# Feature attention in a fused decoder: the mixing cut into halves that stand between single heads, and the maxima's rows turned two heads earlier

## What is computed

```python
qh = layernorm(x).reshape(B, 8, 8, 256)          # B = 32
kh = vh = ctx.reshape(B, 8, 8, 256)
a  = einsum('bhdq,bhdk->bhqk', qh, kh) * 8 ** -0.5
p  = softmax(a, axis=-1)
y  = einsum('bhqk,bhdk->bhdq', p, vh).reshape(B, 64, 256)
x  = x + selu(einsum('oc,bct->bot', W, y))
```

## Time and profile before

| | us |
|---|---|
| median of 3 runs | 1336.93 |
| lowest, highest | 1335.71, 1339.19 |
| the profiled execution | 1332.79 |
| its span, first to last instruction | 1330.7 |
| mean granted TensorE clock | 0.974 |

### The profile page before, as it was taken

One profiled execution on the slowest core, in us unless ns is written; L12 is line 12 of the kernel. 1 busy time (PEld: TensorE's weight loads), 2 busy tenths in 40 slices (PEclk: granted clock), 3 DMA queues, 4 the chain that ended last, 5 costly groups with the idle time before them and its releaser, 6 DMA issues. The chain is left out here.

```text
span 1330.7 us, 27523 instructions
## 1 busy us (share of the span) xinstructions
PE 1215.3 (91%) x9976; PEld 963.9 (72%) x9976; DVE 958.9 (72%) x1862; ACT 709.2 (53%) x1475; POOL 454.5 (34%) x537
## 2 busy tenths in 40 slices
PE   4999988988888779798899999999997999999998
PEld 3677764444444557697677878788786899999998
DVE  5899986888887376887567778677775668555555
ACT  2778763777778546000466565656653463333332
POOL 1444642354553224565552423323240301112210
PEclk8999997999999988899999999999999999999999
DMA  5111161133231210000400000000000300000001
GB/s 173 36 36 37 46 147 32 41 80 95 77 94 35 55 60 0 1 0 13 135 9 4 4 8 4 8 4 8 4 1 9 87 25 25 25 25 25 1 1 64
DMA packets 58660, 51.04 MB, mean 38 GB/s; under 512 B 9064, under 2 KB 50888, under 8 KB 58184
## 3 DMA queue, kind: packets, MB, share of 16 engines
q1 hardware_dynamic: 58574, 49.88, 13.4%
HBM read 37.93 MB, written 11.53 MB: 37 GB/s over the span
## 5 line engine op out<-in xcount | busy, mean ns | idle before, releaser
L842 DVE TENSOR_REDUCE fa_neg_max<-psum 128x2 f32<-128x512 f32 x256 | 163.6, 685 | 35.6 <-PE psum L1015 34.7
L901 ACT ACTIVATE fa_probs<-psum 128x1024 f32<-128x1024 f32 x128 | 130.3, 1020 | 45.5 <-PE psum L1020 44.9
L1872 PE MATMUL psum<-mo_xT_high,mo_w_high 128*128 128x256 f32 x512 | 145.2, 284 | 3.0 <-DVE mo_xT_low L2706 2.8
L1872 PE MATMUL psum<-mo_xT_low,mo_w_high 128*128 128x256 f32 x512 | 144.9, 283 | 0.0
L1872 PE MATMUL psum<-mo_xT_high,mo_w_low 128*128 128x256 f32 x512 | 144.2, 282 | 0.0
L2538 ACT ACTIVATE mo_silu<-psum 128x256 f32<-128x256 f32 x128 | 49.0, 384 | 155.0 <-PE psum L1872 155.0
L2672 DVE TENSOR_TENSOR mo_mid<-mo_silu,psum 128x256 f32<-128x256 f32 x128 | 53.6, 419 | 92.8 <-ACT mo_silu L2538 92.7
L1015 PE MATMUL psum<-stacks_k_stack,stacks_q_stack 48*128 48x256 bf16 x512 | 93.5, 287 | 16.7 <-DVE fa_neg_max L842 7.7
L2008 POOL TENSOR_TENSOR ga_probs<-ga_probs,ga_top 128x1024 f32<-128x1024 f32 x16 | 30.5, 1905 | 203.6 <-DVE ga_top L2162 203.6
L1872 PEld LDWEIGHTS psum<-mo_xT_high,mo_w_high 128*128 128x128 f32 x512 | 97.0, 189 | 3.4 <-DVE mo_xT_low L2706 3.0
L1872 PEld LDWEIGHTS psum<-mo_xT_low,mo_w_high 128*128 128x128 f32 x512 | 97.2, 190 | 0.0
(11 more groups left out here) (434 smaller groups left out, 3548.0 us busy)
## 6 DMA issues: line engine op xcount, KB each, us to landing
k_parts<-da_k_parts SPq DMA_DIRECT2D x96, 64.0 KB, 2.0
stacks_k_stack<-k_parts SPq DMA_DIRECT2D x32, 192.0 KB
q_parts<-stacks_parts SPq DMA_DIRECT2D x48, 64.0 KB, 2.0
stacks_q_stack<-q_parts SPq DMA_DIRECT2D x32, 96.0 KB
x<-in_x SPq DMA_DIRECT2D x4, 512.0 KB, 7.7
da_context<-in_ctx SPq DMA_DIRECT2D x4, 512.0 KB, 7.9
stacks_q_stack<-q_parts SPq DMA_DIRECT2D x32, 64.0 KB
fa_context<-in_ctx SPq DMA_DIRECT2D x16, 128.0 KB, 2.2
```

The costliest lines, as they stand in the source:

```text
L842: nc.vector.tensor_reduce(neg_max[:, b, :, head_at(h)], ps[:, h % 2, :].rearrange("p (q k) -> p q k", q=2), AX.X, ALU.max, negate=True).th ...
L901: nc.scalar.activation(probs[:, g].rearrange("p h k q -> p h (k q)"), ps[:, 2 + 2 * (g % 2):4 + 2 * (g % 2), :], ACT.Exp).then_inc(exp_don ...
L1872: done = nc.tensor.matmul(out, lhsT[i], rhs[j], start=start and k == 0, stop=stop and k == 2)
```

## The change

- TensorE: `heads` (two heads) becomes `head` (one), so that a step may stand between any two. `mix` is called for one half of the contraction (k) at a time, and a head stands between the two halves. The new order of a turn, with A to H the eight half mixes: H0, A (last tile, b 1, first four heads, k 1), H1, B, H2, C, `turn_max(t, 1)`, H3, H4, `turn_mixed(t - 1, 1)`, H5, H6, line 1093's transposes, H7, D, H8, E, H9, `turn_max(t + 1, 0)`, F, H10, G, H11, projection, H12, `turn_mixed(t, 0)`, H13, H14, transposes of the context, H15, H.
- The projection now also waits for the rows of maxima of the next tile (`max_rows_ready`), `turn_max(t + 1, 0)` for `mixed_c_ready` in place of `channels_read`, and the context's transposes for `channels_read`.
- VectorE: `divide(t - 1, 1)` moves from behind H3's maxima to behind H5's, `row_stats` from behind H5's to behind H9's.
- ScalarE: `take_mixed(t, 0)` and `max_to_rows(t + 1, 0)` move ahead of `exponentials(t, 1, 1)`, and `below`, `above` and `exp_below` behind it.
- GpSimd: the SELU of tile t - 2 comes first in a turn, in place of that of tile t - 1 in the middle; `split` moves from the turn's start to between the two `split_max`.

```diff
-                        if g == 1 and b == 0 and valid(t - 1):
+                        if g == 2 and b == 0 and valid(t - 1):
                             divide(t - 1, 1)
-                        if g == 2 and b == 0 and valid(t - 2):
+                        if g == 0 and b == 1 and valid(t - 2):
                             row_stats(t - 2)
...
                     exponentials(t, 1, 0)
+                    take_mixed(t, 0)
+                if valid(t + 1):
+                    max_to_rows(t + 1, 0)
+                if valid(t):
+                    exponentials(t, 1, 1)
                 if valid(t - 1):
                     act.wait_ge(projected, t)
...
-                if valid(t):
-                    exponentials(t, 1, 1)
-                    take_mixed(t, 0)
-                if valid(t + 1):
-                    max_to_rows(t + 1, 0)
-                if valid(t - 1):
                     act.wait_ge(selu_parts, t)
...
             def turn(t, ring, rounds, valid):
-                if valid(t + 3) and started(t, 1):
-                    split(t + 3, ring(3), rounds(3))
                 if isinstance(t, int) and t == -1:
                     pool.sem_inc(split_done, 1)
                     clear_values()
+                if valid(t - 2):
+                    add_selu(t - 2)
                 if valid(t + 1):
                     split_max(t + 1, 0)
...
+                if valid(t + 3) and started(t, 1):
+                    split(t + 3, ring(3), rounds(3))
                 if valid(t + 1):
                     split_max(t + 1, 1)
+                if isinstance(t, int) and t == TILES:
+                    add_selu(t - 1)
...
+            def mix(tile, slot, b, half, k):
+                if k == 0:
+                    pe.wait_ge(exp_done, 8 * tile + (4 * b + 2 * half + 2))
+                    if half == 0:
+                        if b or started(tile, 1):
+                            pe.wait_ge(mixed_ready, 2 * tile + b)
+                        pe.wait_ge(values_ready, tile + 1)
+                for c in range(4):
+                    h = 4 * half + c
+                    done = nc.tensor.matmul(ps[32 * c:32 * c + 32, 6, half * E:(half + 1) * E], values[:, slot, k, 8 * b + head_at(h), :],
+                                            probs[:, h // 2, h % 2, k, :], start=(k == 0), stop=(k == 1), skip_group_check=True)
+                if k == 1:
+                    done.then_inc(mixed_done, 1)
...
+                head(0, 6)
                 if valid(t - 1):
                     if valid(t):
                         pe.wait_ge(max_rows_ready, 2 * t + 2)
...
+                head(0, 7)
+                if valid(t):
+                    mix(t, ring(0), 0, 0, 0)
+                head(1, 0)
+                if valid(t):
+                    mix(t, ring(0), 0, 0, 1)
+                head(1, 1)
                 if valid(t + 1):
                     if isinstance(t, int) and t == -1:
                         pe.wait_ge(loaded, 32)
                     if valid(t - 1):
-                        pe.wait_ge(channels_read, t)
+                        pe.wait_ge(mixed_c_ready, t)
                     elif valid(t):
                         pe.wait_ge(max_rows_ready, 2 * t + 2)
                     turn_max(t + 1, 0)
-                heads(1, 2)
+                if valid(t):
+                    mix(t, ring(0), 0, 1, 0)
+                head(1, 2)
+                if valid(t):
+                    mix(t, ring(0), 0, 1, 1)
+                head(1, 3)
+                if valid(t - 1):
+                    pe.wait_ge(mixed_c_ready, t)
+                    if valid(t + 1):
+                        pe.wait_ge(max_rows_ready, 2 * t + 3)
+                    nc.tensor.matmul(ps[:, 7, E:2 * E], w_out[:], mixed_c[:], start=True, stop=True).then_inc(projected, 1)
+                head(1, 4)
                 if valid(t):
                     turn_mixed(t, 0)
+                head(1, 5)
+                head(1, 6)
```

More of the change, by code:

```diff
@@ L1051, in turn @@
             def turn(t, ring, rounds, valid):
-                def heads(b, g):
-                    for r in range(LANES):
-                        h, beside = 2 * g + r, 2 * g + 1 - r
-                        if valid(t + 1):
[L1057 to L1073, removed]
@@ new lines, in head @@
+                def head(b, h):
+                    g, beside = h // LANES, h + 1 - 2 * (h % LANES)
+                    if valid(t + 1):
+                        if (b, h) == (0, 0) and started(t + 1, RING):
+                            pe.wait_ge(stacked[ring(1)], LOADS * rounds(1))
+                        if not isinstance(t, int) or 8 * b + h >= 2 or t + 1:
+                            pe.wait_ge(max_taken, 16 * (t + 1) + (8 * b + h - 1))
+                    if valid(t) and h % LANES == 0:
+                        if g == 0:
+                            pe.wait_ge(max_stacked[b], 16 * LANES * (t + 1))
+                        if not isinstance(t, int) or 8 * t + 4 * b + g >= 2:
+                            pe.wait_ge(exp_done, 8 * t + (4 * b + g - 1))
+                    for half in range(2):
+                        if valid(t + 1):
+                            taken = largest(ring(1), b, h, half)
+                        if valid(t):
+                            done = score(ring(0), b, beside, half)
+                    if valid(t + 1):
+                        taken.then_inc(max_scored, 1)
+                    if valid(t) and h % LANES:
@@ L1074, in heads @@
                         done.then_inc(scored, 1)
-                heads(0, 0)
+                head(0, 0)
                 if valid(t - 1):
-                    mix(t - 1, ring(-1), 1, 1)
+                    mix(t - 1, ring(-1), 1, 0, 1)
+                head(0, 1)
+                if valid(t - 1):
+                    mix(t - 1, ring(-1), 1, 1, 0)
+                head(0, 2)
+                if valid(t - 1):
+                    mix(t - 1, ring(-1), 1, 1, 1)
                 if valid(t):
@@ L1081, in turn @@
                     turn_max(t, 1)
-                heads(0, 1)
+                head(0, 3)
+                head(0, 4)
                 if valid(t - 1):
                     turn_mixed(t - 1, 1)
-                heads(0, 2)
+                head(0, 5)
+                head(0, 6)
                 if valid(t - 1):
@@ L1094, in turn @@
                     done.then_inc(mixed_turned, 1)
-                heads(0, 3)
+                head(0, 7)
                 if valid(t):
-                    mix(t, ring(0), 0, 0)
-                heads(1, 0)
-                if valid(t - 1):
-                    pe.wait_ge(mixed_c_ready, t)
-                    nc.tensor.matmul(ps[:, 7, E:2 * E], w_out[:], mixed_c[:], start=True, stop=True).then_inc(projected, 1)
-                heads(1, 1)
+                    mix(t, ring(0), 0, 0, 0)
+                head(1, 0)
                 if valid(t):
-                    mix(t, ring(0), 0, 1)
+                    mix(t, ring(0), 0, 0, 1)
+                head(1, 1)
                 if valid(t + 1):
@@ L1118, in turn @@
                     pe.wait_ge(max_rows_ready, 2 * t + 3)
+                    if valid(t - 1):
+                        pe.wait_ge(channels_read, t)
                     for k in range(2):
@@ L1121, in turn @@
                     done.then_inc(values_psum, 1)
-                heads(1, 3)
+                head(1, 7)
                 if valid(t):
-                    mix(t, ring(0), 1, 0)
+                    mix(t, ring(0), 1, 0, 0)
             keep_clock(core, 2, 3)
```

13 lines of the change are left out of this document (12 added, 1 removed).

## The result

| | before | after |
|---|---|---|
| median, us | 1336.32 (4 runs) | 1351.64 (4 runs) |
| lowest, highest | 1332.84, 1339.19 | 1344.78, 1361.40 |
| ratio after to before | | 1.0133, 95% interval 1.0100 to 1.0166 |
| profiled execution, its span | 1332.79, 1330.7 | 1344.78, 1342.7 |

The change makes the kernel slower: 15.3 us by the medians, 13 to 22 by the interval; +26 was forecast. The same kernel, run again, gave 1.0170 (1.0144 to 1.0196), +22.7 us. So the step is about 20 us. One execution of a kernel further down (the changed one with both single edits) ran at a granted clock of 0.835 and took 1400.59 us where the others took 1336 to 1344; it is left out of the ratios, and since the profile is of that execution, no turn is read for that kernel.

The account below looks back on a forecast made before the run. Waits between engines, none of them full, were taken as the bound: a turn of 15.38 us against 13.65, 14 x 1.73 = 24.2, plus 2 at the edges, +26 on 1336.93 gives 1363 us; range 1350 to 1371.

Parts of the forecast that it names:

- the third rival: Half mixes on TensorE cost 0.55 in place of 0.67 each: turn 14.8 us, +17, 1354 us; chance 0.13.
- Half mixes at 0.90: Turn's start on TensorE: head, half mix, next head takes 0.90 us; each cut of a mix costs 0.24.
- `turn_mixed` at +3.47, H5 at +4.17: Behind H4: `turn_mixed` waits for ScalarE's copy of mix C until 3.47 us after H0; H5 follows 0.70 later.
- H7 at +6.26 behind `divide`: Line 1093's transposes behind H6 wait for `divide`, now behind H5's reduction: H7 at 6.26 us, 1.19 of it waiting.
- `turn_max` to a mix at 0.26: Behind H9 on TensorE: from `turn_max` to half mix F, unseen in the trace, taken as 0.26 us between 0.21 and 0.32.
- The projection at +11.38 behind the maxima's rows: Behind H11: projection waits for rows that ScalarE makes after copying mix G, starting at 11.38 us in place of 10.68.
- H at +14.81, the next H0 0.57 later: Turn's end: half mix H waits for H13's reduction, reciprocal and product until 14.81 us; next H0 at 15.38.
- Edges: Turns -1, 0 and 15, outside the 14 full turns: together 2 us more, between 0 and 4.
- Moves that cost nothing: Moved steps off the chain, such as exponentials, `row_stats` and SyncE's stores; H0's 0.31 us wait for the maxima's DMA goes.
- Faster: Halves end VectorE's hunger and the turn falls to TensorE's own 12.4 us: -17.5, 1320 us; chance 0.06.
- No change: Turns keep 13.6 us, waits being made up elsewhere or cut steps not meeting as laid out: 1337 us; chance 0.05.
- A further wait: Another wait, on an exponential or the loop's branch, of 0.6 us a turn: +8, 1371 us; chance 0.10.

Follow-up runs that it names:

- both single edits: Changed kernel with ScalarE's rows of maxima ahead of its copy of the mixed rows, and the divided rows' transposes behind H7: ratio 1.0057, +7.6 us.

## Why the prediction was right, and where its sizes were off

The sign, the mechanism and the new waits were right; the turn was forecast at 15.38 and is 15.08, which at 14 turns is 4.2 us of the forecast's excess. The times alone would not show that. The first median, 1351.64, lies only 1.6 above the lower end of the range, below the 1358 to 1368 of the forecast as laid out and nearer to the third rival's 1354 than to 1363, and the turn of 15.08 lies halfway between that rival's 14.8 and 15.38. That the first median fell inside the range owes something to luck; what decides for the chain is that its links stand in the trace one by one. Step by step, from H0 = 298.43:

1. **Half mixes at 0.90.** H1 and H2 follow at 0.90 and 0.89; the same interval stands at every half mix between two heads. The rival of halves at no extra cost (0.55 a half) is out, by 0.89 where it wanted 0.78; the kernel with whole mixes shows what the cuts take from the turn. The Trainium skill's rule that a change of tiling drains TensorE (TensorEngine Tiling, Key Properties) agrees with the 0.89; its rule on early weight loads (TensorE: Matmul & The Clock Gate, Step-by-step: what each phase is for), on which that rival stood, doesn't show between these tilings.
2. **`turn_mixed` at +3.47, H5 at +4.17.** It started at +3.46 (301.89); H5 came at +4.05, since the step costs 0.59 and not 0.70. I had read 0.70 from the earlier trace rows, where the head waited for VectorE's bank as well: where normalise was moved out of the way on the order of before, the same step takes 0.59 too. The same error stands in step 7: 0.23 in the two places.
3. **H7 at +6.26 behind `divide`.** It came at +6.14, so the chain through reduction, reciprocal and product was right. The wait was too large in my account, 1.19 (0.9 to 1.2 as the sign to look for) against 0.78 here and 10.4 us in 14 turns: H6 follows H5 not by 0.23 but by 0.58, since it waits until ScalarE has read the scores of H2 and H3 (the 0.19 at 303.06, a wait on an exponential that I had not laid out), and what I called a wait was partly that. It changes nothing in the sum, as `divide` ends last in both. Setting the transposes behind H7 shows `divide` as the cause, and that 0.40 of it can be had back.
4. **`turn_max(t + 1, 0)` at +8.62.** It started at +8.52, behind GpSimd, as laid out.
5. **`turn_max` to a mix at 0.26.** 306.95 to 307.05 is 0.10. This term was mis-sized: I took a value between 0.21 and 0.32, and no row of before bounded it from below. Why the step is so short, no run shows.
6. **The projection at +11.38 behind the maxima's rows.** At +11.10, all of the difference being that of steps 2 and 5. Its wait is 0.64 in place of 0.70, and H12's reduction comes 1.66 behind H11's in place of 1.68. Swapping ScalarE's two instructions shows that this wait is worth 0.70 a turn.
7. **H13 at +13.06:** +12.64, with the second 0.12 of `turn_mixed`.
8. **H at +14.81, the next H0 0.57 later.** +14.35, and then 0.73. I had not counted these 0.16. In loop turns H15 to the next H0 takes 1.26, in turns written out 1.13; but the written-out turns last 15.07 as well, since H9 to H10 and H11 to H12 each take 0.06 more in them.

Together: -0.11 (step 2) - 0.16 (step 5) - 0.12 (step 7) - 0.07 (small differences in the other links) + 0.16 (step 8) = -0.30 a turn.

**Edges.** 21.8 - 14 x 1.43 = 1.8 us against 2. **The sum.** Feature attention is 21.8 to 23.4 us longer for the 26 forecast, and the whole kernel 15 to 23: what remains between these lies in the other stages, whose code is the same and which differ between executions (the cause of that is open).

**Moves that cost nothing.** The DMA wait at H0 is gone, as forecast. What missed is VectorE's idle time for `largest`: over 50 was forecast, and 38.9 is measured. I had put all of the longer turn down as idle; nearly half of it is the single reductions' own 0.69 in place of 0.60, by the two rows of the page above.

**The rivals.** *Faster* fell by its own condition: the waits of steps 3, 4 and 6 were not hidden. *No change* fell on the turn of 15.08. *Halves at no extra cost* fell in step 1. *A further wait* did not show in the turn: H6's wait on an exponential is hidden behind `divide`, and loop turns and written-out turns last the same 15.07; only the turns around the loop's entry and its jump back last 15.15 to 15.21.

## What to carry to other kernels

Where no engine is full, lay out one turn as a chain of links and ask of every moved step what its inputs' last producer is doing just then: two ScalarE instructions in the wrong order cost 0.70 a turn here, nearly as much as the cuts of four mixes (0.37) and a missing head (0.40) together. To feed a starving engine more evenly gains nothing when each of the smaller intervals is still longer than its work (0.90 for 0.60). Take the price of a step from a row where nothing else waits there, and don't add up what single edits give back: 1.47 in single edits was 1.18 together, and the same cuts cost 1.10 on one order and at most 0.37 on another.

## What the runs showed that I had not expected

- VectorE's normalise (`tensor_scalar`, fp32, SBUF to SBUF) took 0.40 us in the kernel before, and 0.69 as the median, up to 0.79, where it began beside GpSimd's SELU (fp32 `tensor_tensor` of the same size); moved away it took 0.40 again. The Trainium skill (SBUF — State Buffer, Who interferes with whom) says that a `tensor_scalar` whose operands allow a two-port mode contends with GpSimd for a shared pair of ports, and that the one that issues second blocks until the first is through. The trace agrees: wherever a GpSimd operation still had more than 0.25 us to run when normalise began, normalise ended 0.15 us (0.148 to 0.150) behind that operation's end, nine times in the kernel with GpSimd's new order alone and four times in the changed kernel. Once, where GpSimd's operation is shown to begin 0.03 behind normalise, it was the same; GpSimd's spans are rough. At 309.95 it ends at 310.63, and GpSimd at 309.87 + 0.61 = 310.48. So not the whole 0.40 follows the wait, only the last 0.15. And where GpSimd has less than 0.25 us left, nothing is lost. That is why the change hardly paid for this, although its normalise stands beside the SELU too: its median is 0.405, with 0.548 the longest. Here GpSimd is done 0.20 behind normalise's start (two timelines of the changed kernel):

```profile
300.36 0.41 DVE L119 TENSOR_SCALAR fa_rows<-x,fa_mean,fa_rstd 128x256 f32 x1
```

```profile
299.95 0.61 POOL L988 TENSOR_TENSOR fa_scaled_exp<-fa_exp_below,fa_slope 128x256 f32<-128x256 f32 x1
```

- In a loop turn the first head comes 0.73 us behind its half mix, where any other head comes 0.57 behind one; in turns written out it comes 0.60 behind. What TensorE's sequencer does there I did not part, and the turn as a whole is no longer for it.
- The stage behind feature attention, the same code in all kernels, took between 166.8 and 176.4 us in the profiles from which turns are read. What sets that wasn't looked into; it means that an effect of 10 us is read from the turn, not from one span.
